# Two operations of the stages that finish the attention, moved from VectorE to GpSimd

## The reference

```python
x = _layernorm(x + _L0_attn_ref(x, ...))     # 32 heads of 16, causal, 1024 tokens, and an adapter
x = _layernorm(x + _L0_ffn_ref(x, ...))      # lookup in 128 slots, top 8, gated
x = _layernorm(x + _L1_attn_ref(x, ...))     # 32 heads over 8 key heads, causal
x = _layernorm(x + _L1_ffn_ref(x, ...))      # SwiGLU, 512 -> 1376 -> 512

# the end of _L0_attn_ref: softmax(q k) v, plus the adapter's own attention, then the projection
y = jnp.einsum('bhqk,bhkd->bhqd', attn, v)
y = y + jnp.einsum('bhqk,xhkd->bhqd', ascores, av)
return jnp.einsum('btc,oc->bto', y.transpose(0, 2, 1, 3).reshape(B, T, C), w_proj)

def _layernorm(x):
    m = jnp.mean(x, axis=-1, keepdims=True); v = jnp.var(x, axis=-1, keepdims=True)
    return (x - m) / jnp.sqrt(v + 1e-5)
```

## Time and profile before

| | |
|---|---|
| runs | 1001.0, 1001.11, 1004.68 us; median 1001.11 |
| profiled execution, its own time | 1001.68 us |
| span of its trace | 1000.0 us |
| PE busy | 914.7 us, 91% of the span |
| DVE busy | 648.2 us, 65% |
| ACT busy | 519.6 us, 52% |
| POOL busy | 286.4 us, 29% |
| mean granted clock of PE | 0.937 of full |
| finish of layer 0 | from 399.7 to 444.0 us of the span |
| finish of layer 1 | from 818.4 to 863.1 us |

### The profile page before, as it was taken

How to read it: one execution, slowest core, us unless ns; L and a number is a source line. 1 busy time by engine, 2 the same in 40 slices (tenths; PEclk the granted TensorE clock), 3 DMA queues, 4 the chain that set the end, 5 groups by cost and what they waited for, 6 DMA issues and landing times. The chain is left out here.

```text
span 1000.0 us, 15159 instructions
## 1 busy us (share of the span) xinstructions
PE 914.7 (91%) x5334; PEld 505.8 (51%) x5334; DVE 648.2 (65%) x1151; ACT 519.6 (52%) x1160; POOL 286.4 (29%) x527
## 2 busy tenths in 40 slices
PE   6897989999999998989689799999999889799997
PEld 4575853434444432865366334343444338577766
DVE  5954447877778760874736678787787418454464
ACT  4441322776767666222734147677776652367630
POOL 2666041223223221024247123222223221013200
PEclk9997985999999999987889789999999999899999
DMA  9331061122212110300014401011110010412001
GB/s 325 97 111 63 1 150 29 52 55 54 66 50 64 38 50 1 106 1 0 1 61 126 116 22 41 26 37 39 40 26 3 2 42 1 151 68 72 14 32 53
DMA packets 50029, 57.14 MB, mean 57 GB/s; under 512 B 8928, under 2 KB 39712, under 8 KB 49952
## 3 DMA queue, kind: packets, MB, share of 16 engines
q1 hardware_dynamic: 48320, 55.75, 18.5%
q10 hardware_dynamic: 1632, 0.39, 0.2%
HBM read 43.41 MB, written 12.32 MB: 56 GB/s over the span
## 5 line engine op out<-in xcount | busy, mean ns | idle before, releaser
L1026 DVE TENSOR_REDUCE mx<-psum 128x1 f32<-128x512 f32 (+3 forms) x640 | 370.8, 631 | 116.4 <-PE psum L891 72.3
L886 PE MATMUL psum<-arena_s 96*128 96x512 bf16 (+3 forms) x768 | 228.2, 352 | 10.3 <-PEq L246 5.9
L972 ACT ACTIVATE arena_p<-psum 128x512 f32<-128x512 f32 (+1 forms) x384 | 185.0, 591 | 93.1 <-PE psum L911 61.4
L911 PE MATMUL psum<-arena_s 99*128 99x512 bf16 (+3 forms) x768 | 204.3, 335 | 8.4 <-ACT arena_p L972 3.3
L972 ACT ACTIVATE arena_x<-psum 128x128 f32<-128x128 f32 (+2 forms) x384 | 134.0, 439 | 87.7 <-PE psum L911 64.8
L886 PEld LDWEIGHTS psum<-arena_s 96*128 96x128 bf16 x768 | 71.5, 100 | 125.5 <-DVE mx L1026 70.2
L911 PEld LDWEIGHTS psum<-arena_s 99*128 99x128 bf16 x768 | 66.9, 98 | 100.0 <-ACT arena_p L972 34.0
L1077 POOL TENSOR_SCALAR_AFFINE_SELECT arena_p<-arena_p 128x256 f32<-128x256 f32 x128 | 50.9, 408 | 204.1 <-ACT arena_p L972 204.1
L891 PE MATMUL psum<-maskb,ident_b 128*128 128x128 bf16 (+1 forms) x384 | 97.5, 254 | 0.0
L261 PE MATMUL psum<-x_h,w 128*128 128x512 f32 x224 | 86.5, 449 | 11.6 <-DVE w L497 8.4
L929 PE MATMUL psum<-arena_p,v_grp 128*32 128x512 f32 (+1 forms) x768 | 90.7, 592 | 0.0
(11 more groups left out here) (210 smaller groups left out, 1186.1 us busy)
## 6 DMA issues: line engine op xcount, KB each, us to landing
arena_s<-q_parts SPq DMA_DIRECT2D x32, 192.0 KB, 2.9
arena_s<-k_parts SPq DMA_DIRECT2D x96, 64.0 KB, 2.3
ff_raw<-in_w_in SPq DMA_DIRECT2D x11, 512.0 KB, 3.5
arena_s<-q_parts SPq DMA_DIRECT2D x32, 128.0 KB, 2.9
arena_w<-in_w SPq DMA_DIRECT2D x12, 256.0 KB, 6.5
q_parts<-arena_p SPq DMA_DIRECT2D x24, 128.0 KB
ff_wd_raw<-in_w_down SPq DMA_DIRECT2D x1, 2560.0 KB, 11.5
k_parts<-arena_p SPq DMA_DIRECT2D x18, 128.0 KB
```

Source lines behind the costliest of these rows:

```text
L886: last = pe.matmul(psum[:, bank, width * n:width * n + width], q_st[0:KS, b % NS, 512 * r + P * i:512 * r + P * i + P], k_st[0:KS, g % NK, ...
L911: pe.matmul(psum[:, 2 * (n % 2) + t, o:512], k_st[0:KM, g % NK, at:at + P], q_st[0:KM, u % NS, 512 * r + o:512 * r + 512], start=True, sto ...
L972: act.activation(pr[n % NP_RING][:, t, o:512], psum[:, 2 * (n % 2) + t, o:512], ACT.Exp, scale=scale).then_inc(exp_ready, 1)
L1026: dve.tensor_reduce(mx[:, b % 2, kc, col:col + 4 * len(heads) - 3:4], src, AX, ALU.max)\
```

## The change

GpSimd does two things that VectorE did. In layer 0 it adds the adapter's output to y, behind a new semaphore y_scaled that VectorE raises after the multiplication. In both layers it applies the norm, behind a new semaphore root_ready that VectorE raises after the reciprocal of the root. The reciprocal stays on VectorE. In layer 1 POOL does this behind the cutting of the two weight pieces. VectorE waits for y_scaled, where it waited for y_ready, before it overwrites the reciprocals.

```diff
+        y_scaled, root_ready = ph.sem("y_scaled"), ph.sem("root_ready")
...
-        if layer == 1:
-            @block.gpsimd
-            def _(pool):
-                for i in range(2):
-                    ff.cut_high(pool, pool.tensor_copy, i)
-                    ff.cut_low(pool, i)
+        @block.gpsimd
+        def _(pool):
+            for i in range(2 if layer == 1 else 0):
+                ff.cut_high(pool, pool.tensor_copy, i)
+                ff.cut_low(pool, i)
+            for s in range(NT + 3):
+                if layer == 0 and s < NT:
+                    pool.wait_ge(y_scaled, s + 1)
+                    pool.tensor_tensor(y[:, s % 2, :], y[:, s % 2, :], y_ad[:, s, :], ALU.add)\
+                        .then_inc(y_ready, 1)
+                if 0 <= s - 3 < NT:
+                    t = s - 3
+                    pool.wait_ge(root_ready, t + 1)
+                    pool.tensor_scalar(x_tok[:, t, :], h[:, t % 2, :], stats[:, t % 2, 6:7], stats[:, t % 2, 8:9],
+                                       ALU.subtract, ALU.mult).then_inc(x_ready, 1)
...
                     if t >= 1:
-                        dve.wait_ge(y_ready, t)
+                        dve.wait_ge(y_scaled if layer == 0 else y_ready, t)
...
-                    if layer == 0:
-                        link(mul)
-                        mul = dve.tensor_tensor(y[:, t % 2, :], y[:, t % 2, :], y_ad[:, t, :], ALU.add)
-                    mul.then_inc(y_ready, 1)
+                    mul.then_inc(y_scaled if layer == 0 else y_ready, 1)
...
-                    norm_apply(dve, link, x_tok[:, t, :], h[:, t % 2, :], stats[:, t % 2, :])\
-                        .then_inc(x_ready, 1)
+                    dve.reciprocal(stats[:, t % 2, 8:9], stats[:, t % 2, 8:9]).then_inc(root_ready, 1)
```

## The result

| | before | after |
|---|---|---|
| median of the runs beside each other | 1001.06 us (1000.17 to 1004.68, 4 runs) | 1009.93 us (1009.09 to 1010.71, 4 runs) |
| ratio, 95% interval | | 1.0076 (1.0050 to 1.0103) |
| profiled execution | 1001.68 us | 1009.43 us |
| span of its trace | 1000.0 us | 1007.6 us |
| DVE busy | 648.2 us | 636.5 us |

What follows compares the result with a forecast made beforehand. PE, busy without a gap, was taken to bound the finishes' middle; 0.45 - 0.40 + 0.25 - 0.95 = -0.65 us gave 1001.0 us from the profiled 1001.68, which lay 0.57 above the median, hence 1000.5 us, range 999.0 to 1003.4.

Steps and rivals of the forecast that it cites:

- Cost of the two operations: On POOL the add was to take 1.39 us and the norm 0.75 us, between 0.61 and 1.39.
- X: The assumed time of one norm on POOL: 0.75 us, the cast's 0.61 plus 0.14, at most 1.39.
- The formulas: Change by norm time: layer 0's finish, the larger of X - 0.47 and 2X - 1.43; layer 1's, 2X - 2.46.
- Middle steps: nothing: In the middle of both finishes PE sets the 4.52 us step and POOL keeps up, so no change.
- Fill of layer 0: +0.45: At the first tiles of layer 0's finish PE waits for POOL's add: 0.45 us longer.
- Last tiles of layer 0: -0.40: DVE is no longer late with tile 5's residual add, so tile 6's matmuls start earlier: 0.40 us shorter.
- Drain of layer 1: -0.95: Last norms run on POOL while DVE does line 1249, so tile 7's transposes start earlier: 0.95 us shorter.
- The slow norm: Rival: the norm takes 2.4 us on POOL, exposed at both finishes' ends; +5.7 us, 1006.8 us; chance 0.05.
- Holding each other up: Rival: every POOL instruction stops DVE for its length in the finishes' steps; +8.8 us, 1009.3 us; chance 0.03.
- The clock: Rival: PE's clock rises elsewhere in the fill and behind each finish; -4 to +4 us; chance 0.08.

Runs made afterwards that it cites:

- e_add_only: The changed kernel with the norm back on DVE, only the adapter's add on POOL: 1000.95 us, ratio 0.9987 to the kernel before.
- e_pool_norm5: The changed kernel with POOL applying the norm of tiles 0 to 4 only, DVE that of tiles 5 to 7: 1004.00 us, ratio 1.0008.
- h_both: Against the kernel before: norm on DVE placed ahead of the residual add, POOL doing the adapter's adds of tiles 2 to 7: 1003.61 us, ratio 1.0006.
- d_price: The kernel before, with POOL doing priced copies and tensor_scalar forms that nobody waits for in the finish of layer 0: 1005.49 us, one run.
- e_norm_only: The changed kernel with the adapter's add back on DVE, only the norm on POOL: 1010.38 us, ratio 1.0062 to the kernel before.

## Why the prediction was wrong

- **Cost of the two operations** is the step that failed. "In form it is nearest to the cast" took the number of tensor inputs for what sets the price, and X = 0.75 us came of it; X measured 2.08. The cast has no arithmetic; a tensor_scalar costs 1.49 us for one step and 2.08 for two. The upper bound of 1.39 us was no bound: it was the price of another operation, and nothing in the trace said that a one-input instruction can't cost more than a two-input one. The only honest upper end among the rows was the 2.39 us of the earlier trace rows, which I kept for a rival at 0.05. The prediction also said that nothing showed whether GpSimd comes near VectorE's rate with one input. The runs now show that this instruction does not: 2.08 us against 0.55.
- **The formulas held.** With X = 2.08 they give 2 x 2.08 - 1.43 = +2.7 us for layer 0 and 2 x 2.08 - 2.46 = +1.7 for layer 1; the first pair of traces says +2.78 and +2.21. In layer 0 the agreement is partly luck: the -1.43 was read from the drain of a trace with a low clock, which hid 0.6 us of the cost, and the fill and the last tiles did not come as summed (below). Of the missing 0.5 us in layer 1, 0.35 is the clock: the transposes of tile 7 took 1.11 us, and 0.76 before. The other 0.14 is a wait that I had not named: h has two buffers, so the residual add of tile 7 waits for POOL's norm of tile 5. It came 38.16 us after the stage's start, and 38.02 before. In layer 0 it is the 2.31 us wait in front of 439.19 above, of which about 0.15 was not hidden by the matmuls.
- **Middle steps: nothing** was right, with PE busy 24.00 of 24.00 us. The slack is nearly used up by the slow norm, though: the step in which the first norm is wanted took 4.61 to 4.62 us in the traces with POOL's norms on the first tiles, and 4.49 to 4.53 in the others; the steps behind it took 4.49 to 4.53 again.
- **Fill of layer 0: +0.45** can't be read off one pair of traces, as the clock there differs from run to run. PE's transposes of y for tile 0 (line 1155 in before) came 2.96 to 2.97 us after the stage's start in four traces with DVE's add and 3.29 to 3.56 in the other four; with POOL's add it was 3.58 to 3.59 in three and 4.12 in the fourth. The first projection matmul came after 6.14 us on average in the eight and after 6.66 in the four: +0.5, close to the forecast. In the pair of before and after the low clock of before hid it (first projection matmul after 6.28 and after 6.12 us).
- **Last tiles of layer 0: -0.40.** From the start of tile 5's matmuls to tile 6's it was 431.94 - 427.74 = 4.20 us before, and 3.85 in e_add_only: -0.35, near what was worked out. In the changed kernel it was eaten, since POOL did the add of tile 7 only behind the slow norm of tile 3 and PE waited 0.28 us for it:

```profile
430.40 1.28 POOL L1140 TENSOR_TENSOR arena_s<-arena_s,arena_w 128x512 f32<-128x512 f32 x1
...
431.74 0.66 PE L1165 MATMUL psum<-ident,arena_s 128*128 128x128 f32 x4 [0.28 <-POOL arena_s L1140]
```

- **Drain of layer 1: -0.95** had the right place and, with the wrong X, the wrong sign: +2.07.
- **Rivals.** The slow norm was priced at 2.4 us and +5.7, and is 2.08 us and +5.0 in the finishes of the first pair, +5.7 on average. Holding each other up is refuted for the changed kernel by e_pool_norm5 and by the instructions themselves: all sixteen norms on POOL took 2.07 to 2.08 us, and DVE's residual adds and statistics kept their 0.69 us. It is not always so: in h_both two of the five norms on DVE that met an add on POOL took 0.95 us in place of 0.55, and in d_price one of five adds on DVE took 0.91 in place of 0.69. The clock was named with a reach of 4 us; the low base of the comparison, some 2 us, may be its work or the chip's. It added to the miss but did not cause it.

## What to carry to other kernels

Before an operation is moved to POOL, have a row of the very instruction with its arithmetic, or measure it where POOL is idle; a copy's price says nothing about a tensor_scalar, which here cost 3.8 times DVE's. In a pipeline in which one full engine sets the pace, an operation moved between two others costs only at the two ends, as long as it fits in the step (here 3.36 us of 4.5). If it is moved at all, move it for the middle tiles and leave the last ones, where it stands alone on the path, to the quick engine. Here even that brought nothing (e_pool_norm5, 1.0008), since the relieved engine was not the one that set the pace. Where runs scatter by 8 us, cut the traces at the stages and compare the stretch that was changed, in more than one pair of traces.

## What the runs showed of the hardware

POOL's tensor_scalar on 128x512 f32: 2.00 to 2.08 us with two steps, 1.49 to 1.58 with one, whether the scalars are constants or lie in SBUF; the same engine adds two tensors of that shape in 1.28 us and copies one in 0.61. So of these two the instruction with one input is the slower one. Four adds on DVE with both inputs in SBUF ran wholly beside POOL's 2.08 us norm in e_norm_only and kept their 0.69 us; two norms on DVE beside an add on POOL in h_both took 0.95 us in place of 0.55. PE's transposes behind a wait of 3.33 us took 1.11 us for four in layer 0 and 0.67 in layer 1; those of tile 7 took 1.11 to 1.12 in every trace with their norm on POOL. The same program took 998.3 to 1006.4 us in 29 runs on one chip, along with a mean granted clock from 0.941 to 0.928.
